# The row copies of q and k into on-chip memory: one repeating copy against separate copies without repetition

## What is computed

```
def attention(x, W_Q, W_K, W_V, W_O):            # x is layer-normalised
    Q, K, V = heads of x @ W_Q.T, x @ W_K.T, x @ W_V.T        # 16 heads of 8
    attn = einsum('bhqd,bhkd->bhqk', Q, K) / sqrt(8)
    bias = slopes[:, None, None] * minimum(pos[None, :] - pos[:, None], 0)
    attn = softmax(where(causal, attn + bias, -inf))
    out = einsum('bhqk,bhkd->bhqd', attn, V)
    return out @ W_O.T
x = x + attention(...)
```

## Time and profile before

| | |
|---|---|
| median of 3 runs | 454.65 us |
| the profiled execution, its span from first to last instruction | 454.7 us |
| TensorE busy | 385.5 us (85%) |
| ScalarE busy | 335.0 us (74%) |
| VectorE busy | 159.0 us (35%) |
| GpSimd busy | 44.9 us (10%) |
| mean granted TensorE clock | 0.938 of full speed |
| bytes moved by DMA | 20.87 MB |

### The profile page before, as it was taken

One profiled execution on the slowest core, in us unless ns is written; L12 is line 12 of the kernel. 1 busy time (PEld: TensorE's weight loads), 2 busy tenths in 40 slices (PEclk: granted clock), 3 DMA queues, 4 the chain that ended last, 5 costly groups with the idle time before them and its releaser, 6 DMA issues.

```text
span 454.7 us, 8117 instructions
## 1 busy us (share of the span) xinstructions
PE 385.5 (85%) x2669; PEld 148.6 (33%) x2669; DVE 159.0 (35%) x447; ACT 335.0 (74%) x460; POOL 44.9 (10%) x65
## 2 busy tenths in 40 slices
PE   4951518609999999999999999999999998797986
PEld 1430102202222222222222222222222265697855
DVE  3752205502323231212130301202102047988875
ACT  1630407507988999999999899899999968687482
POOL 5520000000000000000000000000000015470150
PEclk9995658957999999999999999999999999989999
DMA  8633342111311100000000000000000030000003
GB/s 229 172 107 99 128 170 83 79 80 82 133 81 82 79 27 2 0 0 0 0 1 0 2 1 0 0 0 0 0 0 1 1 94 1 1 2 1 0 2 92
DMA packets 11061, 20.87 MB, mean 46 GB/s; under 512 B 500, under 2 KB 9844, under 8 KB 10244
## 3 DMA queue, kind: packets, MB, share of 16 engines
q1 hardware_dynamic: 11036, 20.53, 13.1%
HBM read 16.34 MB, written 4.19 MB: 45 GB/s over the span
## 4 chain that ended last, share of the span: by engine, by line
PE 55%; DMA 11%; issue 11%; ACT 10%; DVE 9%; SPq 2%; POOL 1%; ACTq 0%; DVEq 0%
PE ps L836 23%; PE ps L819 22%; ACT probs L424 7%; DMA kk<-ks 6%; PE ps L727 4%; DMA ks<-kk 3%; DMA x<-in_x 2%; PE ps L905 2%; ACT x L424 2%; PE ps L844 1%; DVE stats L501 1%; PE ps L722 1%; ACT kk L435 1%; SPq L304 1%; POOL rstd L343 1%
## 5 line engine op out<-in xcount | busy, mean ns | idle before, releaser
L424 ACT ACTIVATE probs<-ps 128x1024 f32<-128x1024 f32 (+3 forms) x240 | 206.9, 916 | 71.3 <-PE ps L819 69.5
L819 PE MATMUL ps<-qq,kk 99*128 (+2 forms) x640 | 157.2, 360 | 45.7 <-DMA kk<-ks 29.4
L836 PE MATMUL ps<-probs,vgrp_area 128*9 128x512 f32 (+3 forms) x960 | 113.4, 545 | 2.7 <-DVE probs L606 1.9
L819 PEld LDWEIGHTS ps<-qq,kk 99*128 (+1 forms) x640 | 49.0, 99 | 198.2 <-issue 151.0
L424 ACT ACTIVATE x<-ps 128x1024 f32<-128x1024 f32 (+2 forms) x80 | 67.5, 882 | 0.7 <-PE ps L819 0.6
L614 DVE COPY ot<-ps 128x512 f32<-128x512 f32 x16 | 11.1, 691 | 156.7 <-PE ps L836 156.7
L343 POOL TENSOR_TENSOR rstd<-veps,neghalf 128x4 f32<-128x4 f32 x16 | 17.1, 1070 | 377.9 <-DVE veps L507 377.9
L606 DVE TENSOR_TENSOR probs<-probs,cs 128x512 f32<-128x512 f32 x36 | 24.8, 689 | 55.9 <-ACT probs L424 55.4
L836 PE MATMUL ps<-x,vgrp_area 128*9 128x512 f32 (+2 forms) x320 | 35.9, 520 | 0.0
L606 DVE TENSOR_TENSOR x<-x,cs 128x512 f32<-128x512 f32 x28 | 19.4, 692 | 38.0 <-ACT x L424 38.0
L836 PEld LDWEIGHTS ps<-probs,vgrp_area 128*9 128x9 f32 x960 | 14.5, 88 | 47.0 <-issue 25.9
(11 more groups left out here) (95 smaller groups left out, 264.0 us busy)
## 6 DMA issues: line engine op xcount, KB each, us to landing
qq<-qs SPq DMA_DIRECT2D x3, 1152.0 KB
kk<-ks SPq DMA_DIRECT2D x9, 384.0 KB
x<-in_x SPq DMA_DIRECT2D x8, 256.0 KB, 3.9
kk<-in_krows SPq DMA_DIRECT2D x4, 432.0 KB
qq<-in_qrows SPq DMA_DIRECT2D x4, 432.0 KB
qs<-qq SPq DMA_DIRECT2D x4, 384.0 KB, 9.0
ks<-kk SPq DMA_DIRECT2D x4, 384.0 KB, 13.0
out_y<-x SPq DMA_DIRECT2D x4, 256.0 KB, 2.3
```

The lines of the kernel that those rows point to most:

```text
L424: nc.scalar.activation(slot[:, 2 * u:2 * u + 2, w0:CH], ps[:, b:b + 2, w0:CH], ACT.Exp).then_inc(exp_done, 1)
L819: ins = nc.tensor.matmul(ps[:, 2 * score_buffer(c, n) + v, w0:CH], kk[0:ROWS, bass.ds(head + (H * CH * (kb // TPC) + P * (kb % TPC)), P)], ...
L836: ins = nc.tensor.matmul(ps[32 * v:32 * v + V1, 6, w0:CH], vgrp[:, kb, V1 * v:V1 * (v + 1)], probs_slot(i)[:, v, w0:CH], start=(i == 0), s ...
```

## The change

One loop over the three row blocks takes the place of the repeating copies. For each block it issues one copy of the 24 rows of q and three copies of the same 8 rows of k, with no repeating dimension. The number of copies for each call goes from 4 to 12, and so does the count that the waiting engine looks for. Bytes, sources, destinations and the places in SP's order are the same.

```
-        QK_LOADS = 16 * (PARTS + 1)
+        QK_LOADS = 16 * (PARTS + PARTS * PARTS)
...
             def rows_from_dram(n, h0, h1, done):
                 sp.wait_ge(parts_out[n], 32)
                 a, size = block_cols * n + h0 * CH, (h1 - h0) * CH
-                q_part = qs[n, :, :, h0:h1].rearrange("j d h t -> (j d) (h t)").unsqueeze(0).broadcast_to([PARTS, PARTS * HD, size])
-                sp.dma_start(qq[0:PAIR_ROWS, a:a + size], q_part).then_inc(done, 16)
                 for i in range(PARTS):
                     r = PARTS * HD * i
-                    k_part = ks[n, i, :, h0:h1].rearrange("d h t -> d (h t)").unsqueeze(0).broadcast_to([PARTS, HD, size])
-                    sp.dma_start(kk[r:r + PARTS * HD, a:a + size], k_part).then_inc(done, 16)
+                    q_part = qs[n, :, :, h0:h1].rearrange("j d h t -> (j d) (h t)")
+                    sp.dma_start(qq[r:r + PARTS * HD, a:a + size], q_part).then_inc(done, 16)
+                    k_part = ks[n, i, :, h0:h1].rearrange("d h t -> d (h t)")
+                    for j in range(PARTS):
+                        sp.dma_start(kk[r + HD * j:r + HD * (j + 1), a:a + size], k_part).then_inc(done, 16)
```

## The result

The changed kernel took 441.29 us (median of 4 runs, 439.75 to 445.29) against 454.9 us before (median of 4, 453.18 to 455.25): a ratio of 0.971 with a 95% interval of 0.966 to 0.976. It is faster, by 13.6 us. The forecast was 424, the range 419 to 456: direction and range hold, but 13.6 us came of the 30.5 forecast. In what follows, one execution over 1.5% above the fastest of its kernel (it occurs once, in e2) is left out of the ratio.

A forecast was written before the change was run, and what follows sets the result against it. Mostly PE and ACT inside attention, with PE waiting on row copies (29.4 us in two waits, 13.8 us idle). Entering chunk 1 29.0 us earlier plus 1.5 us of clock, 454.7 minus 30.5, gave 424 us; range 419 to 456.

The forecast's parts named there:

- I take 16.5, since those copies are the nearest in kind: Row copies: each engine was priced at 16.5 GB/s, as on the constant rows, giving 14.9 us a chunk.
- 27 and 16.5: Row copies: bounds in GB/s for one engine's speed, giving 9.1 and 14.9 us a chunk.
- R = 15: Row copies: R is the us that one chunk's rows need, 29 before and 15 forecast.
- the sum: Start to chunk 1: PE passes at 72.9, not 101.89, saving 29.0 us; plus 1.5 of clock, 30.5 us.
- The first rival: Row copies: engines writing adjacent partitions together crowd the destination, so no gain, 452.5 us; chance 0.22.
- the three crowded cases (452.5, 434 and 468 us): Row copies crowded at the destination: without gain 452.5 (chance 0.22), in between 434 (0.13), slower 468 us (0.11).
- Hidden, as before: Rows of chunks 2 and 3: 15 us each, hidden behind chunk 1's attention of over 50 us.
- The number of engines: Row copies: the largest number up to 16 dividing the outermost dimension; 12 for 24 rows, 8 for 8, before 3.
- The issues: On SP: 12 issues a call instead of 4, at 0.5 us each (range 0.33 to 0.71), 6.0 us a call.
- First score at 39.5: Start of attention, chunk 0: first heads' rows land at 39.5, so PE starts then instead of at 44.10.
- No wait into chunk 1, and 1.5 us of clock: Chunk 0 to chunk 1, near 73: the wait vanishes and full clock saves 1.5 us (bounds 0 and 2.2).
- everything after that shifted by about 30 us and not changed: Profile after PE passes into chunk 1: all later work about 30 us earlier, otherwise the same.

The follow-up runs named there:

- e2: Changed kernel with SP waiting until the rows of chunk n-1 have landed before issuing those of chunk n (n = 2, 3); median 434.4 us, ratio 0.954.
- e5: Measuring version of the changed kernel: SP waits for chunk 1's rows, then chunks 2 and 3 run q copies alone, then k copies alone; 434.89 us, one run.
- e6: Same measurement as e5, but with the copies of e1 onto every third partition; 430.94 us, one run.
- e1: Changed kernel with the same copies written to every third partition instead of adjacent ones; 430.32 us, ratio 0.947.
- e8: e1 with the constant rows of chunk 2 issued after the rows of chunk 1 instead of at the start; 423.72 us, ratio 0.932.
- e9: e8 with SP waiting for the rows of chunk n-1 before issuing those of chunk n (n = 2, 3), as in e2; 420.14 us, ratio 0.925.
- e7: Same measurement as e5, but every copy, q's too, has 8 rows and goes onto every ninth partition; 432.81 us, one run.
- e3: Changed kernel with only the q copy taken apart (three copies of 24 rows), k keeping its repeating copies; 453.76 us, ratio 0.999 against the kernel before.

## Why the prediction was right or wrong

**The step that failed** is "I take 16.5, since those copies are the nearest in kind". An engine in the k copies gave 61/7.7 = 7.9 GB/s and one in the q copies 142/10.6 = 13.4 (e5), both onto adjacent partitions; onto every third, one in the k copies gave 133/7.7 = 17.3 (e6). The constant rows, 27 adjacent rows on nine engines at 16.5 GB/s each, did not show how low it could go. Both bounds, 27 and 16.5, lay above the real price; only the rivals went below. From issue to landing the rows of a chunk took 25.1 and 25.4 us (chunk 1 in e2 and e5) and 29.2 (chunk 2 in e2), where the forecast had 18.9 for chunk 1 (53.9 to 72.8, R = 15).

Nearly the whole miss lies in chunk 1. PE passed at 85.50, not 72.9, and the rows had been issued at 54.33, close to the 53.9 forecast. They took 31.2 us in place of 18.9. Of the 12.3 us more, 5.7 are run-ahead (31.2 against 25.4 in e5), for which the sum had no term, and 6.6 the price of the copies. The rest of the miss in time, 441.29 against 424, is the 1.5 us of clock that did not come back, and the 3.1 us by which the two profiled executions lie further apart than the medians.

Chunk 0 came out near the forecast, PE going on at 52.80 and not 51, partly by luck: the issues were quicker (4.0 us a call, not 6.0) and started 1.9 us earlier, which made up for slower data.

**The first rival**, a crowded destination, had the right direction: 8-row copies onto adjacent partitions ran at 61 GB/s and 24-row copies at 142 (e5), and the rows of a chunk took 25.1 and 29.2 us with issue and landing (e2). I gave it 0.22, less than half of the forecast's chance. What the times of the three crowded cases (452.5, 434 and 468 us) were worked out from is shown by no run; they were my estimates, and the kernel took 441.29. The 452.5 is 11 us too high, and most of that arose in chunk 0. Its rows took 22.7 us from first issue (30.08) to use (52.80), where the 29.2 us of e2's chunk 2, from the same start, would have ended near 59. The same copies of chunk 0 took 23.7 us in e5 (28.80 to 52.49) and 25.8 in e2 (30.82 to 56.61), so single traces differ by 3 us here too. Why all three stay under the 29.2 of e2's chunk 2 I did not settle. Engines out of step would explain it, which is not shown. In time the 434 came nearest.

**Chunk 1** then lost part of what chunk 0 had won: 31 us instead of 25, by run-ahead (e2 and e5). The prediction had the rows of chunks 2 and 3 as "Hidden, as before". They were off the path, but not free: they cost the rows of chunk 1 5.7 us. SP had issued chunk 1's rows first, and still about 1.1 MB of later rows moved beside them.

**The number of engines** was right: 0.77 of 16 while both kinds move, 0.48 of 16 or 7.7 for the k copies alone, 0.66 or 10.6 for q (e5). So was the hint that the repeating dimension held it at three.

**The issues** were mis-sized on the harmless side: 0.29 to 0.33 us, not 0.5. The doubled price, 0.70 us for q, came back in e1 with destinations on every third partition. The long issues of SP did not all go, though the forecast had said so: one of 7.41 us is left (6.89 and 10.01 before).

**First score at 39.5**: it came at 39.93, but not for my reason. In e8 the rows were issued 4.9 us earlier still and the first score came no sooner, so what follows the flag holds it there, not the rows. In the changed kernel this is likely: its wait too ends on "issue", 6.2 us after the flag. Before, the rows were the last to come and hid that.

**No wait into chunk 1, and 1.5 us of clock**: neither came (the granted clock was 0.50 behind the wait before (101.89 to 103.80) and with the change, 85.50 to 87.00). In e9 both did, and there the kernel is 34.5 us faster than before, with three further edits (every third partition, later constant rows, the wait on SP).

**"everything after that shifted by about 30 us and not changed"**: not changed is right, since what follows PE's pass into chunk 1 takes 352.5 us against 352.8. The shift is 16.4 us.

## What to carry to other kernels

Read the share and the GB/s of a window together, and divide. Here twelve engines in place of three moved 129 GB/s and not four times 82: engines that filled adjacent partitions crowded each other (7.9 GB/s each in e5's k copies), and a stride of three in the destination partitions cut the nine k copies from 19.9 to 11.1 us, at twice the issue price (5.8 us for the nine against 3.0). Where a later transfer stands beside one that somebody waits for, try holding it back: here the rows that ran ahead cost those of chunk 1 5.7 us onto adjacent partitions (e5) and 2.9 onto every third (e6).

## What the runs showed of the hardware that I had not expected

- Copies of 8 rows of 16 KB: 61 GB/s onto adjacent partitions, 133 onto every third, 166 onto every ninth, with nearly the same number of busy engines (0.46 to 0.48 of 16) and the same source rows (e5, e6, e7).
- Three engines slowed from 0.60 to about 1.3 us a row when nine others wrote q rows beside them (e3): the kernel was no faster with 0.72 of 16 engines busy than with 0.19.
- Rows of later chunks, issued early, moved about 1.1 MB while chunk 1's were awaited and cost those 5.7 us (the changed kernel against e5).
- A copy to adjacent partitions took about 0.3 us to issue, one to every third or ninth mostly 0.60 to 0.73, about as long as one with a repeating source (0.71).
- PE started its first score 5.6 us after the flag for its branch had been written, with the trace naming nothing that it waited for (e8).
